# A transformer block on one core: weight halves moved to GpSimd and the mixture's bookkeeping put in another order

## The reference, cut to what matters

```python
scores = softmax(xf @ gate_w.T)
top_vals, top_idx = top_k(scores, 2)
w_dense = zeros((T, 8)).at[arange(T)[:, None], top_idx].set(top_vals)
h = einsum('td,ehd->teh', xf, W1)
y, g = split(h, 2, axis=-1)
eo = einsum('teh,edh->ted', y * silu(g), W2)
z = einsum('te,ted->td', w_dense, eo)
z = z + _gated_mlp(xf, Ws1, Ws2)
x = x + tanh(g_ffn[1]) * z
```

## Time and profile before

| | us |
|---|---|
| runs | 1020.51, 1022.22, 1024.47 |
| median | 1022.22 |
| profiled execution | 1018.67 |
| its span | 1016.9 |
| PE busy | 945.3 (93%) |
| DVE busy | 769.9 (76%) |
| ACT busy | 576.2 (57%) |
| POOL busy | 398.3 (39%) |

### The profile page before, as it was taken

How to read it: one execution, slowest core, us unless ns; L and a number is a source line. 1 busy time by engine, 2 the same in 40 slices (tenths; PEclk the granted TensorE clock), 3 DMA queues, 4 the chain that set the end, 5 groups by cost and what they waited for, 6 DMA issues and landing times.

```text
span 1016.9 us, 23135 instructions
## 1 busy us (share of the span) xinstructions
PE 945.3 (93%) x6523; PEld 809.0 (80%) x6523; DVE 769.9 (76%) x2336; ACT 576.2 (57%) x1344; POOL 398.3 (39%) x571
## 2 busy tenths in 40 slices
PE   5999999999999878999999999997999995999995
PEld 4666666766766557999999999986898885999995
DVE  3777777777766336788888888889888878888884
ACT  1688888888887633443443444433555542666663
POOL 1011111111111002544453454345675751777776
PEclk9999999999999989999999999999999997999998
DMA  7765765764740250110010001000123545778785
GB/s 219 181 145 127 168 136 115 170 145 108 173 115 1 65 176 28 31 52 27 27 53 27 27 27 54 27 7 1 43 93 113 172 131 177 124 125 134 125 133 69
DMA packets 91812, 98.42 MB, mean 97 GB/s; under 512 B 14992, under 2 KB 85472, under 8 KB 91744
## 3 DMA queue, kind: packets, MB, share of 16 engines
q1 hardware_dynamic: 77504, 79.11, 29.9%
q0 software_dynamic: 13680, 17.84, 10.3%
q10 hardware_dynamic: 560, 0.66, 0.2%
HBM read 30.18 MB, written 59.01 MB: 88 GB/s over the span
## 4 chain that ended last, share of the span: by engine, by line
PE 55%; DVE 6%; issue 1%; POOL 1%; ACT 1%; DMA 0%; POOLq 0%; DVEq 0%; ACTq 0%
PE c_out L1373 3%; PE c_turned L1384 3%; PE c_hidden L1377 3%; PE c_mlp L1377 3%; PE c_hidden L1379 3%; PE c_hidden L1378 3%; PE c_cross L1373 3%; PE c_mlp L1378 3%; PE c_mlp L1379 3%; PE m_gate L2215 3%; PE m_gate L2217 3%; PE m_gate L2216 2%; PE c_scores L1373 2%; PE m_router L2137 1%; PE c_turned L1373 1%; PE m_gate L2160 1%
## 5 line engine op out<-in xcount | busy, mean ns | idle before, releaser
L1720 POOL DMA_INDIRECT out<-early_weights,aim x71 | 110.5, 1556 | 57.1 <-DMA out<-early_weights,aim 27.9
L1189 ACT ACTIVATE f_hidden<-c_hidden,f_b 128x256 f32<-128x256 f32 x128 | 53.7, 471 | 66.6 <-PE c_hidden L1379 66.6
L1377 PE MATMUL c_mlp<-f_w_hi,f_hidden_hi 128*128 128x256 f32 x256 | 80.6, 315 | 7.5 <-DVE f_hidden_lo L1307 7.5
L1695 POOL DMA_INDIRECT sorted_rows<-m_z,slot_i x64 | 69.6, 1088 | 36.4 <-issue 18.5
L1377 PE MATMUL c_hidden<-y2T_hi,f_w_hi 128*128 128x256 f32 x256 | 77.7, 304 | 0.0
L1379 PE MATMUL c_hidden<-y2T_hi,f_w_lo 128*128 128x256 f32 x256 | 72.8, 284 | 0.0
L1378 PE MATMUL c_hidden<-y2T_lo,f_w_hi 128*128 128x256 f32 x256 | 72.7, 284 | 0.0
L1379 PE MATMUL c_mlp<-f_w_hi,f_hidden_lo 128*128 128x256 f32 x256 | 72.4, 283 | 0.0
L1378 PE MATMUL c_mlp<-f_w_lo,f_hidden_hi 128*128 128x256 f32 x256 | 72.3, 283 | 0.0
L784 PE MATMUL ps_probT<-ident,prob 128*77 128x128 f32 x512 | 67.1, 274 | 3.7 <-ACT prob L511 3.2
L628 DVE TENSOR_REDUCE mx<-ps_scores 128x8 f32<-128x616 f32 x64 | 50.9, 795 | 25.4 <-PE ps_scores L714 25.3
(11 more groups left out here) (355 smaller groups left out, 3115.3 us busy)
## 6 DMA issues: line engine op xcount, KB each, us to landing
sorted_rows<-no_row SPq DMA_DIRECT2D x15, 2340.0 KB, 12.2
m_z<-sorted_rows SPq DMA_DIRECT2D x71, 130.0 KB
early_weights<-expert_chunks SPq DMA_DIRECT2D x8, 640.0 KB, 4.6
combT<-combineT_all SPq DMA_DIRECT2D x16, 256.0 KB, 2.3
slT<-slots_all SPq DMA_DIRECT2D x16, 256.0 KB, 2.5
out<-x_all SPq DMA_DIRECT2D x8, 512.0 KB, 6.1
x_all<-x SPq DMA_DIRECT2D x15, 256.0 KB, 11.4
f_w_stage<-L_xattn_w SPq DMA_DIRECT2D x4, 512.0 KB, 3.7
```

Source lines behind the costliest of these rows:

```text
L1189: last = act.activation(hf[:, q % 2, j, :], psH[:, q % 2, j, :], ACT.Relu, bias=fb1[:, c_:c_ + 1])
L1377: pe.matmul(out, lh, rh, start=start, stop=False, skip_group_check=shared)
L1695: pool.indirect_dma_start(out=sorted_rows[:, :], in_=zn[:, b % 3, t, :], in_offset=None, out_offset=bass.IndirectOffsetOnAxis(ap=slot_i[:, ...
L1720: pool.indirect_dma_start(out=self.out[:, :], in_=xo[:, i % XO, :], in_offset=None, compute_op=ALU.add, out_offset=bass.IndirectOffsetOnAx ...
```

## The change

1. `expert_lo(e)` goes from DVE to POOL. It and `expert_hi(e)` now stand in the round after block e's number (stage 1) and no longer in the third.
2. `flags` leaves the table. `tile_flags` becomes a generator with six stops, and DVE runs one piece of it at the end of each of the first seven tiles.
3. The order of all steps in the table is new, and so are some stages: `scatter` goes from stage 0 to stage 2, `later_rstd` from 0 to 2, `table` from 2 to 1, `down(1)` and `down(2)` from 3 to 2. The highest stage is now 2, so there are 10 rounds and no longer 11.

```diff
-        order = [(SHARED, "hidden_lo", 2), (SHARED, "table"), (ROUTE, "zf_out", 1), (AHEAD, "scatter"),
...
-                 (ROUTE, "hidden_lo", 1), (ROUTE, "tanh"), (AHEAD, "later_rstd"), (ROUTE, "silu", 1), (LATE, "flags")]
+        order = [(ROUTE, "logits"), (SHARED, "hidden_hi", 1), (SHARED, "silu", 2), (ROUTE, "hidden", 0),
+                 (ROUTE, "weights"), (ROUTE, "up", 0), (SHARED, "scatter"), (AHEAD, "rows_in"), (AHEAD, "turn_z", 0),
+                 (ROUTE, "hidden", 1), (ROUTE, "up", 1), (SHARED, "hidden_hi", 2), (ROUTE, "silu", 0),
+                 (ROUTE, "places"), (AHEAD, "zf_out", 0), (ROUTE, "table"), (SHARED, "down", 0), (ROUTE, "tanh"),
+                 (ROUTE, "expert_hi"), (AHEAD, "turn_z", 1), (AHEAD, "z_lo"), (ROUTE, "ranks"),
+                 (ROUTE, "hidden_lo", 0), (SHARED, "result"), (ROUTE, "silu", 1), (ROUTE, "expert_lo"),
...
             def scatter(b):
...
+            def expert_lo(e):
+                pool.wait_ge(weh_done.sem, e + 1)
+                pool.tensor_tensor(el[:, e, :], self.stage_expert(e), eh[:, e, :].bitcast(F32), ALU.subtract).then_inc(wel_done.sem, 1)
...
-            def expert_lo(e):
-                dve.wait_ge(weh_done.sem, e + 1)
-                dve.tensor_tensor(el[:, e, :], self.stage_expert(e), eh[:, e, :].bitcast(F32), ALU.subtract).then_inc(wel_done.sem, 1)
...
             def tile_flags():
-                step = lambda n: dve.wait_ge(t_step.sem, n)
+
+                def step(n):
+                    dve.wait_ge(t_step.sem, n)
...
+                yield
                 step(17)
...
-            def flags_last(b):
-                if b == NBLK - 1:
-                    tile_flags()
...
+            flags_program = tile_flags()
             for i in range(XT + 1):
...
+                next(flags_program, None)
```

More of the change, by code:

```diff
@@ L1593, in phase_d @@
         AHEAD, ROUTE, SHARED, LATE = range(4)
-        order = [(SHARED, "hidden_lo", 2), (SHARED, "table"), (ROUTE, "zf_out", 1), (AHEAD, "scatter"),
[L1596 to L1602, removed]
-                 (ROUTE, "hidden_lo", 1), (ROUTE, "tanh"), (AHEAD, "later_rstd"), (ROUTE, "silu", 1), (LATE, "flags")]
+        order = [(ROUTE, "logits"), (SHARED, "hidden_hi", 1), (SHARED, "silu", 2), (ROUTE, "hidden", 0),
[4 more added lines that the diff above has]
+                 (ROUTE, "hidden_lo", 0), (SHARED, "result"), (ROUTE, "silu", 1), (ROUTE, "expert_lo"),
+                 (SHARED, "down", 1), (ROUTE, "hidden_lo", 1), (SHARED, "down", 2), (ROUTE, "hidden", 2),
+                 (ROUTE, "later_stats"), (AHEAD, "top_two"), (ROUTE, "hidden_lo", 2), (SHARED, "later_rstd"),
+                 (AHEAD, "zf_out", 1), (ROUTE, "hidden_hi", 0), (AHEAD, "z_hi"), (ROUTE, "up", 2)]
         def added(eng, i):
@@ L1701, in later_rstd @@
                     rstd(b // 2 + 2)
-            unrolled(pool, order, dict(scatter=scatter, later_rstd=later_rstd), NBLK)
+            unrolled(pool, order, dict(scatter=scatter, expert_lo=expert_lo, later_rstd=later_rstd), NBLK)
             for j in range(XO):
@@ L2063, in table_last @@
                     tile_table()
-            def flags_last(b):
-                if b == NBLK - 1:
-                    tile_flags()
             unrolled(dve, order, dict(z_lo=later(z_lo), top_two=later(top_two), weights=weights, places=places, hidden=hidden, hidden_lo=hidden_lo,
-                                      result=result, expert_lo=expert_lo, later_stats=later_stats, table=table_last, flags=flags_last), NBLK)
+                                      result=result, later_stats=later_stats, table=table_last), NBLK)
             def aims(i):
```

## The result

The changed kernel took 1030.82 us in the median (1028.63 to 1034.54), the kernel before 1022.22. The ratio is 1.0085, with a 95% interval of 1.0069 to 1.0102: **8.6 us slower**. The forecast was 1027.3 with a range of 1017 to 1035. Direction and range hold; the loss is 8.6 us and not 5.1.

The account below looks back on a forecast made before the run. PE was taken to bound rounds and tiles, with DVE the path between them and POOL's adds near their own pace. Terms +4.2 - 2.8 + 3.7 = +5.1 us on 1022.2 gave 1027.3 us, range 1017 to 1035.

Parts of the forecast that it names:

- Part 1: Full rounds: low halves on POOL delay rows for PE, while DVE's relief is worth nothing; +4.2 us, from +2 to +7.
- The chain ahead of block 4: On POOL, three low halves, two scatters and `rstd` end at 766.5; block 4's rows come late, PE stalls 3.3 us.
- Blocks 3 and 6: Rounds: rows 0.6 us too late for PE at block 3, and 0.3 us more lost at block 6.
- the row of 1772 ns: Profile row: a two-input DVE operation, usually 682 ns, took 1772 while POOL's two-input operation ran; basis for delaying the table.
- Part 2: End of rounds to first tile: 5.9 us less, partly taken back by clock and POOL; -2.8 us, from -6 to +1.
- The hold-up by POOL: DVE's table after block 7's `places`: `expert_lo(7)` on POOL beside it makes DVE stand; +1.6 us (0 to 3.2).
- the clock's term: Last 36 `down(7)` matmuls partly run at half clock after PE stood still; +1.5 us (0 to 3) on 4.4.
- Part 3: Flags in the tiles: first add 11.4 us later, then POOL's 1.86 us pace regains 7.7; +3.7 us, from +2 to +5.
- the first term: The term for low halves on POOL in the rounds: +4.2 us, from +2 to +7.
- faster: Rival: POOL keeps under its cover, rows never late, DVE not held up, clock stays up; -5.4 us, 1016.8; chance 0.14.
- no change: Rival: only a 2 us stall at block 4, -5.9 at the rounds' end, +2.5 for adds; -1.4, 1020.8; chance 0.26.
- much slower: Rival: low halves of 4.98 us make POOL the bound of the rounds; about +14 us, 1036; chance 0.14.

Follow-up runs that it names:

- second trace: Each kernel run once more unchanged, both on one chip, one execution each: kernel before 1020.46 us, changed kernel 1023.93 us.
- first trace: The originally profiled execution of each kernel: kernel before 1018.67 us (median 1022.22), changed kernel 1032.0 us (median 1030.82).
- third trace: A further run of either kernel, unchanged: kernel before 1021.33 us; changed kernel, timed again beside two repairs of it, 1030.69 us, ratio 1.0088.

## Why the prediction was right, and where it was off

**Part 1, forecast +4.2.** The low half took 2.95 us (3.24 taken from a row of another shape). The chain ahead of block 4 did as told: in the second trace `rstd` ended at 764.34 instead of 766.5. Of these 2.2 us, 0.8 are the start of the chain (all of that trace lies 0.7 us earlier), 1.1 the three low halves (3.1 with their gaps, not 3.5) and 0.6 the two blocks of row writes; `rstd` took 0.3 more. PE waited 2.04 us, 3.3 had been forecast. (In the first trace PE doesn't wait for these rows at all, since late signals had held it up before.) Blocks 3 and 6 cost next to nothing.

The step that failed is the sentence that what DVE gives up is worth nothing in the rounds and that it gets from 13.4 down to 11.9 us. I had the row of 1772 ns and used it only for the table. The hold-up came beside seven of eight low halves, and where it made `places` late PE waited: 0.43 us in the second trace, in a round 0.6 us too long; 0.85 in the first, and 1.7 of clock behind it. Where the trace is clean the term is 107.87 - 104.61 = +3.3, of which the round with block 4's wait has 2.3. So its closeness to 4.2 is partly luck: the wait was put too high and the hold-up left out. On other chips the term is +6.8 and +8.3; the kernel before lost 1.7 in the one trace of it with late signals.

**Part 2, forecast -2.8.** Measured -0.7, -1.1 and -1.6. The new bound was named rightly, DVE's table ahead of `down(7, 0)`. Two terms were too small. The hold-up by POOL was put at 1.6 on the table; in the second trace it fell on `place_picked` and was 2.5 (2.70 for 0.22), and `places(7)` ended 12.8 us after the logits, not 10.1. (In the first trace it ended as late, but only 1.0 us of that was the hold-up; ACT's last `silu` came with a late signal of 2.45 us.) And the 36 matmuls took 7.0 us, not 4.4 + 1.5, since PE had stood still for longer than the 3.9 us put in and the clock stayed at 0.50 for 25 of them:

```profile
854.00:856.00 2.00, 2.00 (x11) 2.00 (x11) 0.00 (x0) 0.00 (x0) 0.00 (x0) 0.50 0.44 124
```

With the low halves on DVE the hold-up is gone and the clock's term is as forecast: PE stands still for 3.76 us instead of 6.49, the 36 matmuls take 6.0, and the same stretch is 28.68, 4.7 under the kernel before (5.9 had been forecast ahead of the two terms, 4.4 with the clock's).

**Part 3, forecast +3.7.** The first add came 20.5, 18.7 and 20.0 us after the first gate (19.5), then the pitch was 1.86 us. First to last add took 140.3, 138.8 and 139.4 us (137.8): the stalls beside the pitch are 8.6 to 10.1 us, not 7.6. Against 8.07 and 145.45 that makes +7.3, +3.9 and +5.9. The mechanism is shown by the flags alone in the kernel before.

**The sum.** +3.3 - 1.1 + 3.9 = +6.1 between the second trace of the changed kernel and the trace that the forecast was made from (5.6 between the two second traces), against a forecast of +5.1. The 8.6 us of the medians hold, as far as single traces can tell, what the forecast had no term for: late signals. That both times come out inside the range owes something to luck, since against the second trace the first term was 0.9 too high and the second 1.7 too low, and this one was missing. The rival "faster" fell with DVE's hold-ups, "no change" with the first add, and "much slower" with 2.95 us a low half.

## What to carry to other kernels

An engine that is idle isn't free for the taking: here a two-input operation on GpSimd stopped DVE's next one on two SBUF operands until it ended, so count each such operation as time of both engines. Moving work into the gaps of a loop pays only if nobody waits for its last piece; put it where the engine already waits for another, and split it there. When a table of steps, a new home for an operation and a new cut of another come in one change, time them apart: here one of the three was a gain.

## What the runs showed of the hardware

**Late signals.** In nine of fourteen traces ACT and DVE go on some us after PE has done what they wait for. In the first trace of the changed kernel, PE and ACT:

```profile
772.08 0.60 PE L2135 MATMUL m_turned<-ident,m_z 128*128 128x128 f32 x4
...
775.98 0.37 PE L2181 MATMUL m_acc<-s_weights_hi,m_hidden_lo 128*128 128x256 f32 x1 [0.34 <-issue]
...
776.09 0.59 ACT L1760 COPY m_zT<-m_turned 128x512 f32<-128x512 f32 x1 [2.37 <-remote]
```

PE turned the rows by 772.7, ACT copied them out at 776.1, and PE itself stumbled until 775.98, in the middle of a run of `down` matmuls that wait for nobody. "remote" is what the profile writes where it knows no releaser. Whole traces, by their waits (us in total, number, longest), the kernel before (third trace) and the changed one (first):

```profile
ACT m_zT L1756 <- remote: 8.6, 4, 3.2
DVE place L1911 <- remote: 6.4, 2, 5.2
```

```profile
ACT silu L1773 <- remote: 9.9, 4, 3.2
ACT m_zT L1760 <- remote: 7.3, 3, 3.1
ACT m_hidden_hi L1780 <- remote: 5.2, 1, 5.2
DVE place L1911 <- remote: 3.0, 3, 1.7
DVE x_all L1947 <- remote: 3.0, 1, 3.0
```

They all lie in the rounds, the only part in which POOL issues row writes. The four traces from one chip have none, whatever the kernel; the eight from three other chips all have them. For the first trace of either kernel the chip isn't on record: the changed kernel's has them, the other's none. Kernels with the low halves on DVE lost 1.7 to 2.9 us in the rounds there, those with them on POOL (but for the one in the old order) 6.0 to 8.3, against 3.3 without late signals. On the one chip with traces of both kinds the low halves on POOL made the rounds 3.6 to 4.8 us longer (6.5 against 2.9 and 1.7). What holds the signals up was not found, and no kernel was made to try it.

**The clock.** PE stopped for 0.85 us ahead of 796.29, busy on both sides, and the granted clock was 0.50 from 798 to 800; the round behind the stop was 1.66 us longer than 15.56. Ahead of 838.89 the kernel before stopped PE for 1.59 us, with PE busy on both sides too, and kept its clock:

```profile
838.00:840.00 2.00, 1.11 (x9) 1.14 (x10) 2.00 (x6) 1.43 (x3) 1.48 (x2) 1.00 1.01 372
840.00:842.00 2.00, 2.00 (x19) 2.00 (x18) 1.83 (x7) 0.52 (x1) 1.70 (x2) 1.00 1.08 397
```

Nor did the stop of 2.04 us ahead of 766.51 in the second trace of the changed kernel cost any clock. So such a stop has two prices, its own length or (0.85 + 1.66 us for 0.85) about three times that, and no run here tells them apart beforehand.

A good part of what the changed kernel lost is this. In its first trace the clock fell twice in the rounds, the other time behind a stop of 0.75 us at 746.00 with a late signal:

```profile
746.00:748.00 2.00, 2.00 (x12) 1.90 (x12) 1.86 (x3) 1.93 (x5) 1.83 (x2) 0.70 0.00 0
748.00:750.00 2.00, 2.00 (x7) 1.52 (x6) 2.00 (x6) 1.75 (x4) 1.70 (x2) 0.50 0.69 141
750.00:752.00 2.00, 2.00 (x12) 1.69 (x11) 1.79 (x10) 0.33 (x1) 1.39 (x3) 0.95 0.79 320
```

That makes 2 x 1.7 = 3.4 of the 6.8 us by which its rounds were too long. Each of the other four traces of kernels with the new order, the low halves on POOL and late signals has one such fall in the rounds; the traces with the low halves on DVE have none there.
